# Edge stage of a graph-network kernel: every second group's one-hots on ScalarE, and a split first relu in every fourth pair

## The chip, the cores and the metric

The kernel runs on one core of one Trainium2 chip. The metric is the device time of one execution in microseconds (us). Engines are named as in the profile: PE is TensorE's matmuls, PEld its weight loads, DVE is VectorE, ACT is ScalarE, POOL is GpSimd, SP issues DMAs.

## The reference

3125 nodes with 256 features, 50,000 edges with 16 features. After a layer norm and a relu (giving h) comes a message-passing layer, then three graph convolutions, which the change doesn't touch. Cut to the part that it does touch:

```
h = maximum(layernorm(x), 0)
msg_input = concatenate([h[src], h[dst], edge_attr])      # 50000 x 528
hid       = relu(msg_input @ mW1 + mb1)                   # 50000 x 512
messages  = hid @ mW2 + mb2
aggregated = segment_sum(messages, src)                   # 3125 rows
```

Since the second matrix product is linear, the kernel sums hid over the edges of a source node first (the sums of this stage, 512 wide) and multiplies by mW2 once for each node later.

## The kernel before, in words

An earlier stage sorts the edges by source node, in blocks of 128 source nodes, and writes them as 440 tiles of 128 edges. It leaves A = h times the source part of mW1 plus mb1 in SBUF (each as two F32R halves whose sum is the value), and B = h times the target part in DRAM. F32R is the 32-bit type that PE reads with reduced precision; F32 operands go in full.

The edge stage (`edge_mlp`) works on pairs of tiles; both tiles of a pair belong to one source block. There are 220 pairs, and 110 quads of four tiles. For a pair p:

- one-hots (`one_hots`, L1188 to 1194): for a whole quad, one DVE is_equal makes `oh`, edge by source node, 128x512. It stands in even iterations, for the quad that PE needs two iterations later. There are four slots.
- turn (L1057): PE transposes the pair's two one-hots and its split edge features into PSUM; ACT copies them out (`turned` L1153, with a read of its accumulator, and `turned_e` L1155).
- edge (L1070): six matmuls with 512 columns sum the edge features' part and A's two halves in PSUM, over two PSUM areas in turns.
- pre (`add_target`, L1196 to 1207): DVE adds the rows of B, which POOL has gathered by indirect DMA, and writes `pre`, 128x1024 (512 for each of the two tiles).
- relus: the first tile's relu is written by ACT as F32 (`hid_whole`, L1161). The second tile's is split: ACT writes it rounded to F32R (`hid_upper`, L1165), and DVE subtracts that from the exact relu (`hid_lower`, `lower_part`, L1213).
- node (L1082): three matmuls sum by source node in `pNode`: the one-hot times `hid_whole` in F32 (L1087, two records of one pass pair each in the trace), times `hid_upper` (L1089) and `hid_lower` (L1091) in F32R.
- sums (`add_pair`, L1217 to 1226): DVE adds `pNode` to the block's running row sums. The block's place comes from a register; registers are loaded for four pairs at once, ahead of the sums in the iterations divisible by four.

All orders are written out by hand as loops over iterations i, one for each engine, and engines meet only by counting semaphores:

```
PE  (L1129): turn(i); edge(i-1); node(i-3)
ACT (L1148): turned(i), turned_e(i); hid_whole(i-2), hid_upper(i-2)
DVE (L1250): [i even: one_hots(i/2+1)]; pre(i-1); hid_lower(i-2); sums(i-4)
```

`pNode` has two buffers, so node(p) waits until sums(p-2) is done (`pe.wait_ge(sums_ready, p)`, L1085). By the loops above, node(i-2) in PE's iteration i+1 thus waits for the last operation of DVE's iteration i, whose first waits for edge(i-1) in PE's iteration i.

Of the kernel before, what the change touches and what calls it, by code (L numbers as in the profile page):

```python
# [5 lines left out]
P = 128  # L6
ALU = mybir.AluOpType
# [937 lines left out]
def edge_mlp(nc, io, dr, keep):  # L945


    with ExitStack() as stack:
# [3 lines left out]
        GRP = 4  # L952
        QUADS = NT // LC
        OHQ = 4
        WHOLE, SPLIT = 3, 2
        rows = g.sb("rows", [P, LCS, LC, ROW])
        rows_i = rows[:, :, :, :].rearrange("p s t w -> p (s t w)").bitcast(I32).rearrange(
            "p (s t w) -> p s t w", s=LCS, t=LC)
# [9 lines left out]
        whole = g.sb("hid_whole", [P, WHOLE, HID])  # L968
        upper = g.sb("hid_upper", [P, SPLIT, HID], F32R)
        lower = g.sb("hid_lower", [P, SPLIT, HID], F32R)  # L970
        ub2 = g.sb("ub2", [P, D])
        iota_i = g.sb("iota_cw_i", [P, CW], I32)
        ends_after = g.sb("ends_after", [P, NW])
        pair_m = g.sb("pair_m", [P, KP])
        col_f = brow[:, 0:2, :].rearrange("p s n -> p (s n)")[:, 0:2 * NT].rearrange("p (q t) -> p q t", q=2)
# [6 lines left out]
        cols_copied = g.sem("cols_copied")  # L982
        rows_in = [g.sem(f"rows_in{n}") for n in range(LCS)]
        b_in = [g.sem(f"b_in{n}") for n in range(BR)]
        oh_ready = g.sem("oh_ready2")
        turn_done = g.sem("turn_done")
        turn_copied = g.sem("turn_copied")
# [2 lines left out]
        whole_ready = g.sem("whole_ready")  # L990
        upper_ready = g.sem("upper_ready")
        lower_ready = g.sem("lower_ready")
        node_done = g.sem("node_done")
        sums_ready = g.sem("sums_ready")
        ub_in = g.sem("ub_in")
# [57 lines left out]
        def _(pe):  # L1053
# [2 lines left out]

            def turn(p):  # L1057
                q, j = divmod(2 * p, LC)
                pe.wait_ge(oh_ready, q + 1)
                if p >= 2:  # L1060
                    pe.wait_ge(turn_copied, p - 1)
                for n in range(2):
                    nc.tensor.transpose(pT[p % 2][:, n * P:(n + 1) * P], oh_upper[:, q % OHQ, j + n, :, 1],
                                        keep.ident16[:, :])
                for n in range(2):
                    last = nc.tensor.transpose(pT[p % 2][0:EW, (2 + n) * P:(3 + n) * P],  # L1066
                                               rows16[:, q % LCS, j + n, 4:4 + EW], keep.ident16[:, :])
                last.then_inc(turn_done, 1)
# [13 lines left out]
            def node(p):  # L1082
                q, j = divmod(2 * p, LC)
                if p >= 2:
                    pe.wait_ge(sums_ready, p)  # L1085
                pe.wait_ge(whole_ready, p + 1)
                mm(pN[p % 2][:, :], oh[:, q % OHQ, j, :].bitcast(F32), whole[:, p % WHOLE, :], start=True, stop=False)  # L1087
                pe.wait_ge(upper_ready, p + 1)
                mm(pN[p % 2][:, :], oh[:, q % OHQ, j + 1, :], upper[:, p % SPLIT, :], start=False, stop=False)  # L1089
                pe.wait_ge(lower_ready, p + 1)  # L1090
                mm(pN[p % 2][:, :], oh[:, q % OHQ, j + 1, :], lower[:, p % SPLIT, :], start=False, stop=True  # L1091
                   ).then_inc(node_done, 1)
# [52 lines left out]

        @block.scalar
        def _(act):
            for i in range(PAIRS + 2):  # L1148
                if i < PAIRS:
                    act.wait_ge(turn_done, i + 1)  # L1150
                    if i >= 2:
                        act.wait_ge(edge_done, i - 1)
                    nc.scalar.activation(turned[:, i % 2, :], pT[i % 2][:, 0:2 * P], ACT.Copy,  # L1153
                                         accum_out=keep.pair_deg[:, i:i + 1])
                    nc.scalar.copy(turned_e[:, i % 2, :], pT[i % 2][0:EW, 2 * P:4 * P]).then_inc(turn_copied, 1)  # L1155
                p = i - 2
                if p >= 0:
                    act.wait_ge(pre_ready, p + 1)
                    if p >= WHOLE:
                        act.wait_ge(node_done, p - WHOLE + 1)  # L1160
                    nc.scalar.activation(whole[:, p % WHOLE, :], pre[:, p % 2, 0:HID], ACT.Relu  # L1161
                                         ).then_inc(whole_ready, 1)
                    if p >= SPLIT:
                        act.wait_ge(node_done, p - SPLIT + 1)
                    nc.scalar.activation(upper[:, p % SPLIT, :], pre[:, p % 2, HID:2 * HID], ACT.Relu  # L1165
                                         ).then_inc(upper_ready, 1)
            act.wait_ge(edge_done, PAIRS)
            act.wait_ge(lists_done, 1)
            for m in range(KP):
                size = min(P, PAIRS - m * P)  # L1170
                nc.scalar.copy(keep.degT[0:size, m, :], pT32[0][0:size, m * P:(m + 1) * P]).then_inc(lists_copied, 1)
            act.wait_ge(lists_done, 2)
            full, size = KT - 1, NT - (KT - 1) * P
            for q in range(2):
                nc.scalar.copy(keep.turned_full(q),
                               pE[1][:, q * HID:q * HID + full * P].rearrange("p (m k) -> p m k", m=full)
                               ).then_inc(lists_copied, 1)
                nc.scalar.copy(keep.turned(q, full)[0:size, :], pE[1][0:size, q * HID + full * P:q * HID + KT * P]
                               ).then_inc(lists_copied, 1)
            act.wait_ge(lists_copied, KP + 4)  # L1180

        @block.vector
        def _(dve):
# [12 lines left out]
            def add_target(p):  # L1196
                dve.wait_ge(edge_done, p + 1)
                for t in (2 * p, 2 * p + 1):
                    dve.wait_ge(b_in[t % BR], 16 * (t // BR + 1))
                if p >= 2:  # L1200
                    dve.wait_ge(whole_ready, p - 1)
                    dve.wait_ge(upper_ready, p - 1)
                    dve.wait_ge(lower_ready, p - 1)
                at_row = (2 * p) % BR
                v.tensor_tensor(pre[:, p % 2, :], pE[p % 2][:, :],  # L1205
                                brow[:, at_row:at_row + 2, :].rearrange("p t n -> p (t n)"), ALU.add
                                ).then_inc(pre_ready, 1)

            def lower_part(p):
                dve.wait_ge(upper_ready, p + 1)  # L1210
                if p >= SPLIT:
                    dve.wait_ge(node_done, p - SPLIT + 1)
                v.scalar_tensor_tensor(out=lower[:, p % SPLIT, :], in0=pre[:, p % 2, HID:2 * HID], scalar=0.0,  # L1213
                                       in1=upper[:, p % SPLIT, :].bitcast(F32), op0=ALU.max, op1=ALU.subtract
                                       ).then_inc(lower_ready, 1)

            def add_pair(p):  # L1217
                if p % GRP == 0:
# [29 lines left out]

            one_hots(0)
            for i in range(PAIRS + 5):  # L1250
                if i % 2 == 0 and i // 2 + 1 < QUADS:
                    one_hots(i // 2 + 1)
                if 0 <= i - 1 < PAIRS:
                    add_target(i - 1)
                if 0 <= i - 2 < PAIRS:
                    lower_part(i - 2)
                if 0 <= i - 4 < PAIRS:
                    add_pair(i - 4)
# [935 lines left out]
```

## Time and profile before

| what | value |
|---|---|
| runs of the kernel | 2032.16, 2037.77, 2036.21 us; median 2036.21 us |
| the profiled execution | 2026.99 us |
| its span, first to last instruction | 2025.3 us |
| edge stage in it | from 546.5 us to about 1213 us |
| node matmuls in it, first and last weight load | 557.2 us and 1211.3 us |
| granted PE clock of the whole span, as a share of the full one | 0.925 |
| granted PE clock from 700 to 1200 us | 1.00 |
| busy in the whole span | PE 89%, DVE 76%, POOL 62%, PEld 61%, ACT 39% |

The profile is one execution, recorded by the hardware. "Busy" leaves out the time in which an engine waits. PE's matmul records overlap, since they are pipelined and their ends are modelled; how long a matmul holds the array is read from the starts of its neighbours and of the weight loads. DVE and ACT instructions also overlap the next one's start by a little, so that the step from start to start is shorter than the duration.

### The profile page before, as it was taken

Reading aid. Unit: us, or ns where it says so; the run is one execution under the profiler, and the core shown is the slowest. Engines: PE = TensorE matmul, PEld = TensorE weight load, DVE = VectorE, ACT = ScalarE, POOL = GpSimd, SP = SyncE. Lnnn points to the kernel's source line nnn. Section 1 sums busy time; section 2 is a strip of 40 time slices with the busy share of each in tenths; the row PEclk is TensorE's granted clock in tenths of the full one; section 3 lists DMA queues with packets and bytes.
Section 4 is the critical chain, followed back from the end, with each engine's and each line's share of the span. In section 5 each row is a group of like instructions: output and inputs, shape, how many; then the busy total and the mean of one; then the engine's idle time right before and its main releaser. Section 6 shows DMA issues by size and latency. Waiting matters only on the chain. (4 is left out here: it accounts for less than half of the span.)

```text
span 2025.3 us, 34940 instructions
## 1 busy us (share of the span) xinstructions
PE 1810.6 (89%) x9004; PEld 1239.8 (61%) x9005; DVE 1544.2 (76%) x4663; ACT 797.6 (39%) x1975; POOL 1256.3 (62%) x1468
## 2 busy tenths in 40 slices
PE   3577877777499999999999998999989999999999
PEld 3344444444255555555555556777758788888887
DVE  8877776777489999999999988999987445445333
ACT  0122222222155566665655555666664222103000
POOL 4777777777788888888888859999977100000000
PEclk7677777888699999999999999999999999999999
DMA  5111111111276666666666696222226233333333
GB/s 166 39 59 50 53 58 52 57 59 58 61 200 198 196 196 194 196 196 196 196 195 195 197 182 172 74 72 73 88 85 199 94 113 121 109 125 110 109 109 111
DMA packets 181291, 254.03 MB, mean 125 GB/s; under 512 B 28876, under 2 KB 144265, under 8 KB 181098
## 3 DMA queue, kind: packets, MB, share of 16 engines
q0 software_dynamic: 48048, 126.51, 22.7%
q1 hardware_dynamic: 104408, 102.03, 16.2%
q10 hardware_dynamic: 28642, 23.25, 3.6%
q8 instruction: 81, 1.33, 0.3%
q14 instruction: 112, 0.92, 0.2%
HBM read 202.22 MB, written 49.37 MB: 124 GB/s over the span
## 5 line engine op out<-in xcount | busy, mean ns | idle before, releaser
L1037 POOL DMA_INDIRECT brow<-B_rows,rows x440 | 470.0, 1068 | 115.2 <-issue 61.5
L393 POOL DMA_INDIRECT src_list<-ring,ring_row x392 | 385.4, 983 | 133.8 <-issue 116.8
L2018 PE MATMUL pO<-F,y 128*128 128x512 f32 x1728 | 427.7, 401 | 0.8 <-DVE y L1822 0.8
L2018 PEld LDWEIGHTS pO<-F,y 128*128 128x128 f32 x1728 | 325.1, 189 | 73.7 <-ACT zT L1911 1.5
L1360 POOL TENSOR_SCALAR src_oh<-iota,src_s 128x128 bf16<-128x128 bf16 x426 | 279.2, 672 | 32.4 <-PE pC L1512 15.8
L1087 PE MATMUL pNode<-hid_whole,oh 128*128 128x512 f32 x440 | 227.4, 598 | 4.2 <-DVE sums L1223 3.7
L1153 ACT ACTIVATE turned<-pC 128x256 fp32r<-128x256 bf16 x220 | 84.4, 384 | 280.4 <-PE pC L1066 280.4
L1376 DVE TENSOR_SCALAR dst_oh<-iota_cw,dst_s 128x458 bf16<-128x458 f16 x568 | 182.5, 370 | 1.6 <-PE pC L1512 1.4
L1512 PE MATMUL pC<-dst_oh,src_oh 128*128 128x458 bf16 x568 | 159.9, 361 | 18.4 <-SPq L1467 11.3
L1089 PE MATMUL pNode<-hid_upper,oh 128*128 128x512 f32 x220 | 174.9, 795 | 0.0
L852 PE MATMUL pP<-U,upto 128*128 128x182 bf16 x385 | 48.9, 277 | 136.4 <-DVE posf L612 136.4
L1205 DVE TENSOR_TENSOR pre<-pC,brow 128x1024 f32<-128x1024 f32 x110 | 134.7, 1225 | 45.2 <-PE pC L1078 41.6
L1078 PE MATMUL pC<-A,turned 128*128 x440 | 168.2, 493 | 0.0
L1078 PE MATMUL pSU<-A,turned 128*128 x440 | 167.1, 491 | 0.0
L1223 DVE SCALAR_TENSOR_TENSOR sums<-sums,going_on,pNode 128x512 f32 x220 | 163.6, 743 | 2.0 <-PE pNode L1091 1.2
L1818 DVE CAST F<-raw 128x512 fp32r<-128x512 uint16 x324 | 126.7, 432 | 32.4 <-PE pO L2018 32.0
L1213 DVE SCALAR_TENSOR_TENSOR hid_lower<-pre,hid_upper 128x512 fp32r<-128x512 f32 x220 | 151.4, 688 | 0.0
L1161 ACT ACTIVATE hid_whole<-pre 128x512 f32<-128x512 f32 x220 | 139.9, 636 | 7.4 <-DVE pre L1205 7.4
L1205 DVE TENSOR_TENSOR pre<-pSU,brow 128x1024 f32<-128x1024 f32 x110 | 134.2, 1220 | 5.1 <-PE pSU L1078 2.1
L1165 ACT ACTIVATE hid_upper<-pre 128x512 fp32r<-128x512 f32 x220 | 136.5, 620 | 0.0
L1595 ACT CAST c_rows<-pC 128x458 uint16<-128x458 f32 x175 | 94.6, 540 | 101.7 <-PE pC L1512 78.8
L852 PEld LDWEIGHTS pP<-U,upto 128*128 128x128 bf16 x385 | 36.0, 110 | 146.4 <-DVE posf L612 134.2
(308 smaller groups left out, 3423.6 us busy)
## 6 DMA issues: line engine op xcount, KB each, us to landing
raw<-C_rows SPq DMA_DIRECT2D x54, 768.0 KB, 4.3
C_rows<-c_rows ACTq DMA_DIRECT2D x175, 114.5 KB, 1.7
raw_first<-C_rows SPq DMA_DIRECT2D x18, 768.0 KB, 4.2
rows<-src_list SPq DMA_DIRECT2D x110, 100.0 KB, 2.8
brow<-B_rows,rows POOLq DMA_INDIRECT x440, 3.8
U_parts<-part_u SPq DMA_DIRECT2D x25, 256.0 KB, 2.0
B_rows<-bst SPq DMA_DIRECT2D x25, 256.0 KB, 2.1
src_list<-ring,ring_row POOLq DMA_INDIRECT x392, 2.2
```

The source lines that it names most:

```text
L393: nc.gpsimd.indirect_dma_start(dr.src_list[:, :, :].rearrange("p t w -> (p t) w"), bass.IndirectOffsetOnAxis(ap=ring_row[:, k % RING, t:t ...
L1037: nc.gpsimd.indirect_dma_start(brow[:, t % BR, :], None, dr.B, bass.IndirectOffsetOnAxis(ap=rows_i[:, m % LCS, j, 1:2], axis=0)).then_inc( ...
L1078: last = mm(to, turned[:, p % 2, n * P:(n + 1) * P], keep.A[:, 2 * HID + k * HID:][:, bass.ds(at[p], HID)], start=False, stop=(k == 1))
L1087: mm(pN[p % 2][:, :], oh[:, q % OHQ, j, :].bitcast(F32), whole[:, p % WHOLE, :], start=True, stop=False)
L1089: mm(pN[p % 2][:, :], oh[:, q % OHQ, j + 1, :], upper[:, p % SPLIT, :], start=False, stop=False)
L1205: v.tensor_tensor(pre[:, p % 2, :], pE[p % 2][:, :], brow[:, at_row:at_row + 2, :].rearrange("p t n -> p (t n)"), ALU.add).then_inc(pre_re ...
L1213: v.scalar_tensor_tensor(out=lower[:, p % SPLIT, :], in0=pre[:, p % 2, HID:2 * HID], scalar=0.0, in1=upper[:, p % SPLIT, :].bitcast(F32), ...
L1223: v.scalar_tensor_tensor(out=keep.sums[:, bass.ds(at[p], HID)], in0=keep.sums[:, bass.ds(at[max(p - 1, 0)], HID)], scalar=keep.going_on[:, ...
L1360: nc.gpsimd.tensor_scalar(src_oh[:, s % SLOTS, :], keep.iota16[:, :], src_s[:, s:s + 1], None, ALU.is_equal).then_inc(src_ready, 1)
L1376: v.tensor_scalar(dst_oh[:, s % SLOTS, :], iota_cw[:, :], dst_s[:, s:s + 1], None, ALU.is_equal).then_inc(dst_ready, 1)
L1512: mm(pC[:, bass.ds(at[s % GRP], CW)], src_oh[:, s % SLOTS, :], dst_oh[:, s % SLOTS, :], start=False, stop=False, skip_group_check=True).th ...
L2018: last = mm(pO[m % 2][half][:, :], y[:, win, part, half * P:(half + 1) * P], F[:, n % FS, :], start=(win == 0 and part == 0), stop=False)
```

## The change

It has three parts, all in `edge_mlp`.

1. Quads with an odd number get their one-hots from ACT. Four instructions (`distances`, two in each of two iterations) write the distance of the edge's source from each column, by the function Abs with the source number as a bias; one instruction on the quad's 512 columns (`own_one_hots`) makes relu(1 - distance) of it. They stand behind ACT's relus in the iterations 3, 0 and 1 modulo 4. DVE keeps the even quads, in the iterations 3 modulo 4.
2. In the pairs 3 modulo 4 the first tile's relu is split as the second's: ACT writes it rounded (`hid_upper_a`), DVE subtracts (`lower_part_a` to `hid_lower_a`), and node has four F32R matmuls in place of one F32 and two F32R.
3. `hid_whole` has two buffers instead of three, and the iota for later use lies in a part of `pre` that the second pair is the first to write.

```diff
-        WHOLE, SPLIT = 3, 2
+        WHOLE, SPLIT = 2, 2
+        BOTH = 4
...
-        iota_i = g.sb("iota_cw_i", [P, CW], I32)
+        iota_i = pre[:, 1, 0:CW].bitcast(I32)
...
             def turn(p):
                 q, j = divmod(2 * p, LC)
-                pe.wait_ge(oh_ready, q + 1)
+                if q % 2:
+                    pe.wait_ge(oh_own, (LC + 1) * (q // 2 + 1))
+                else:
+                    pe.wait_ge(oh_ready, q // 2 + 1)
...
-                pe.wait_ge(whole_ready, p + 1)
-                mm(pN[p % 2][:, :], oh[:, q % OHQ, j, :].bitcast(F32), whole[:, p % WHOLE, :], start=True, stop=False)
+                if p % BOTH == BOTH - 1:
+                    pe.wait_ge(whole_ready, p + 1)
+                    mm(pN[p % 2][:, :], oh[:, q % OHQ, j, :], upper_a[:, :], start=True, stop=False)
+                    pe.wait_ge(lower_a_ready, p // BOTH + 1)
+                    mm(pN[p % 2][:, :], oh[:, q % OHQ, j, :], lower_a[:, :], start=False, stop=False)
+                else:
...
+            def distances(q, t0):
+                act.wait_ge(rows_in[q % LCS], 16 * (q // LCS + 1))
+                if q >= OHQ:
+                    act.wait_ge(node_done, 2 * (q - OHQ) + 2)
+                for t in (t0, t0 + 1):
+                    nc.scalar.activation(oh[:, q % OHQ, t, :], keep.iota[:, :], ACT.Abs,
+                                         bias=rows[:, q % LCS, t, 0:1], scale=-1.0).then_inc(oh_own, 1)
+
+            def own_one_hots(q):
+                act.wait_ge(oh_own, (LC + 1) * (q // 2) + LC)
+                nc.scalar.activation(oh[:, q % OHQ, :, :], oh[:, q % OHQ, :, :].bitcast(F32), ACT.Relu,
+                                     bias=keep.ones[:, 0:1], scale=-1.0).then_inc(oh_own, 1)
...
+                if i == 0:
+                    distances(1, 0)
+                if i % 4 == 3 and (i + 3) // 2 < QUADS:
+                    distances((i + 3) // 2, 0)
+                if i % 4 == 0 and (i + 2) // 2 < QUADS:
+                    distances((i + 2) // 2, 2)
+                if i % 4 == 1 and (i + 1) // 2 < QUADS:
+                    own_one_hots((i + 1) // 2)
...
+            def lower_part_a(p):
+                dve.wait_ge(whole_ready, p + 1)
+                if p >= BOTH:
+                    dve.wait_ge(node_done, p - BOTH + 1)
+                v.scalar_tensor_tensor(out=lower_a[:, :], in0=pre[:, p % 2, 0:HID], scalar=0.0,
+                                       in1=upper_a[:, :].bitcast(F32), op0=ALU.max, op1=ALU.subtract
+                                       ).then_inc(lower_a_ready, 1)
...
-                if i % 2 == 0 and i // 2 + 1 < QUADS:
-                    one_hots(i // 2 + 1)
+                if i % 4 == 3 and (i + 1) // 2 < QUADS:
+                    one_hots((i + 1) // 2)
                 if 0 <= i - 1 < PAIRS:
                     add_target(i - 1)
                 if 0 <= i - 2 < PAIRS:
+                    if (i - 2) % BOTH == BOTH - 1:
+                        lower_part_a(i - 2)
                     lower_part(i - 2)
```

DVE's order, two iterations (i = 8 and 9) before the change. A line number L1192 is the one-hots, L1205 pre, L1213 hid_lower, L1223 sums (its ISA row sets up the register address):

```order
1697 L1192 TENSOR_TENSOR oh<-iota,rows 128x512 [waits node_done,rows_in3]
1698 L1205 TENSOR_TENSOR pre<-pSU,brow 128x1024 [waits whole_ready,upper_ready,b_in7,lower_ready,b_in6,edge_done]
1699 L1213 SCALAR_TENSOR_TENSOR hid_lower<-pre,hid_upper 128x512 [waits node_done,upper_ready]
1700 L80 TENSOR_LOAD pair_at
1701 L1223 ISA [waits sums_ready,node_done]
1702 L1223 SCALAR_TENSOR_TENSOR sums<-sums,going_on,pNode 128x512
1703 L1205 TENSOR_TENSOR pre<-pC,brow 128x1024 [waits whole_ready,upper_ready,b_in1,lower_ready,b_in0,edge_done]
1704 L1213 SCALAR_TENSOR_TENSOR hid_lower<-pre,hid_upper 128x512 [waits node_done,upper_ready]
1705 L1223 ISA [waits sums_ready,node_done]
1706 L1223 SCALAR_TENSOR_TENSOR sums<-sums,going_on,pNode 128x512
```

The same two iterations with the change (its line numbers: L1246 pre, L1262 hid_lower_a, L1254 hid_lower, L1272 sums):

```order
1696 L1246 TENSOR_TENSOR pre<-pSU,brow 128x1024 [waits whole_ready,upper_ready,b_in7,lower_ready,b_in6,edge_done]
1697 L1254 SCALAR_TENSOR_TENSOR hid_lower<-pre,hid_upper 128x512 [waits node_done,upper_ready]
1698 L80 TENSOR_LOAD pair_at
1699 L1272 ISA [waits sums_ready,node_done]
1700 L1272 SCALAR_TENSOR_TENSOR sums<-sums,going_on,pNode 128x512
1701 L1246 TENSOR_TENSOR pre<-pC,brow 128x1024 [waits whole_ready,upper_ready,b_in1,lower_ready,b_in0,edge_done]
1702 L1262 SCALAR_TENSOR_TENSOR hid_lower_a<-pre,hid_upper_a 128x512 [waits node_done,whole_ready]
1703 L1254 SCALAR_TENSOR_TENSOR hid_lower<-pre,hid_upper 128x512 [waits node_done,upper_ready]
1704 L1272 ISA [waits sums_ready,node_done]
1705 L1272 SCALAR_TENSOR_TENSOR sums<-sums,going_on,pNode 128x512
```

The one-hots ahead of pre are gone from the first of the two, and the new subtraction stands between pre and sums in the second.

ACT's order with the change, in the iterations i = 8 and 9 (L1168 distances, L1173 own_one_hots, L1181 and L1183 the copies, L1190 hid_upper_a, L1192 hid_whole, L1196 hid_upper; before, an iteration was the two copies and the two relus):

```order
338 L1181 ACTIVATE turned,pair_deg<-pC 128x256 [waits edge_done,turn_done]
339 L1183 COPY turned_e<-pC 96x256
340 L1192 ACTIVATE hid_whole<-pre 128x512 [waits node_done,pre_ready]
341 L1196 ACTIVATE hid_upper<-pre 128x512 [waits node_done]
342 L1168 ACTIVATE oh<-iota,rows 128x128 [waits node_done,rows_in1]
343 L1168 ACTIVATE oh<-iota,rows 128x128
344 L1181 ACTIVATE turned,pair_deg<-pC 128x256 [waits edge_done,turn_done]
345 L1183 COPY turned_e<-pC 96x256
346 L1190 ACTIVATE hid_upper_a<-pre 128x512 [waits node_done,pre_ready]
347 L1196 ACTIVATE hid_upper<-pre 128x512 [waits node_done]
348 L1173 ACTIVATE oh<-oh,ones 128x512 [waits oh_own]
```

The rows 342, 343 and 348 are added; the next row is the copy for turn(10), whose PE transposes read what row 348 writes.

## Rows read from the trace of the kernel before

**Rows 1.** Stretches: busy time of each engine, granted clock, DMA share and GB/s.
```profile
core 0: us, PE busy (x) PEld busy (x) DVE busy (x) ACT busy (x) POOL busy (x), PEclk, DMA share, GB/s
800.00:900.00 100.00, 100.00 (x477) 59.57 (x475) 93.31 (x120) 60.44 (x170) 82.08 (x89) 1.00 0.68 196
```

**Rows 2.** Waits from 700 to 1200 us: in total, times, longest.
```profile
ACT turned L1153 <- PE pC L1066: 200.6, 169, 1.7
PEld pNode L1087 <- DVE sums L1223: 10.2, 45, 0.7
```

**Rows 3.** Timeline, PE over one iteration: start, us, engine, line, operation.
```profile
902.33 1.02 PE L1087 MATMUL pNode<-hid_whole,oh 128*128 128x512 f32 x2
...
903.42 0.40 PE L1091 MATMUL pNode<-hid_lower,oh 128*128 128x512 f32 x1
...
903.66 0.29 PE L1063 MATMUL pC<-ident,oh 128*128 128x128 bf16 x2
...
903.89 0.38 PE L1076 MATMUL pC<-we_rows,turned_e 96*128 96x512 bf16 x1
...
905.28 1.02 PE L1087 MATMUL pNode<-hid_whole,oh 128*128 128x512 f32 x2
...
906.61 0.28 PE L1063 MATMUL pC<-ident,oh 128*128 128x128 bf16 x2
```

**Rows 4.** Timeline, DVE over an iteration, and the weight loads of the node behind it.
```profile
905.48 1.23 DVE L1205 TENSOR_TENSOR pre<-pC,brow 128x1024 f32<-128x1024 f32 x1 [0.44 <-PE pC L1078]
...
906.62 0.68 DVE L1213 SCALAR_TENSOR_TENSOR hid_lower<-pre,hid_upper 128x512 fp32r<-128x512 f32 x1
...
907.22 0.74 DVE L1223 SCALAR_TENSOR_TENSOR sums<-sums,going_on,pNode 128x512 f32 x1
...
907.88 0.69 DVE L1192 TENSOR_TENSOR oh<-iota,rows 128x512 fp32r<-128x512 f32 x1
...
908.01 0.40 PEld L1087 LDWEIGHTS pNode<-hid_whole,oh 128*128 128x128 f32 x2
...
908.23 1.02 PE L1087 MATMUL pNode<-hid_whole,oh 128*128 128x512 f32 x2
...
908.48 1.22 DVE L1205 TENSOR_TENSOR pre<-pSU,brow 128x1024 f32<-128x1024 f32 x1
```

**Rows 5.** Timeline, the next iteration, whose sums follow a register load.
```profile
909.61 0.69 DVE L1213 SCALAR_TENSOR_TENSOR hid_lower<-pre,hid_upper 128x512 fp32r<-128x512 f32 x1
...
910.29 0.75 DVE L1223 SCALAR_TENSOR_TENSOR sums<-sums,going_on,pNode 128x512 f32 x1
...
911.09 0.30 PEld L1087 LDWEIGHTS pNode<-hid_whole,oh 128*128 128x128 f32 x2 [0.20 <-DVE sums L1223]
...
911.63 0.19 PEld L1089 LDWEIGHTS pNode<-hid_upper,oh 128*128 128x128 f32 x1 [0.24 <-issue]
...
912.52 0.12 PEld L1063 LDWEIGHTS pC<-ident,oh 128*128 128x128 bf16 x2 [0.27 <-issue]
```

**Rows 6.** Timeline, ACT over one iteration.
```profile
904.09 0.38 ACT L1153 ACTIVATE turned<-pC 128x256 fp32r<-128x256 bf16 x1 [1.18 <-PE pC L1066]
...
904.72 0.64 ACT L1161 ACTIVATE hid_whole<-pre 128x512 f32<-128x512 f32 x1
...
905.25 0.62 ACT L1165 ACTIVATE hid_upper<-pre 128x512 fp32r<-128x512 f32 x1
```

**Rows 7.** ACT's groups by shape, whole span: count, busy us, mean ns, idle before.
```profile
L1153 ACT ACTIVATE turned<-pC 128x256 fp32r<-128x256 bf16 x220 | 84.4, 384 | 280.4 <-PE pC L1066 280.4
...
L442 ACT ACTIVATE part_u<-pT,ub 128x128 f32<-128x128 f32 x100 | 28.5, 367 | 185.5 <-PE pT L892 185.5
...
L490 ACT ACTIVATE A<-resid,nmr,rstd 128x256 f32<-128x256 f32 x25 | 15.0, 600 | 2.4 <-DVE nmr L677 2.4
...
L1171 ACT CAST sums<-pC 128x128 bf16<-128x128 f32 x1 | 0.2, 246 | 0.0
```

More of the change, by code:

```diff
@@ L970, in edge_mlp @@
         lower = g.sb("hid_lower", [P, SPLIT, HID], F32R)
+        upper_a = g.sb("hid_upper_a", [P, HID], F32R)
+        lower_a = g.sb("hid_lower_a", [P, HID], F32R)
         ub2 = g.sb("ub2", [P, D])
-        iota_i = g.sb("iota_cw_i", [P, CW], I32)
+        iota_i = pre[:, 1, 0:CW].bitcast(I32)
         ends_after = g.sb("ends_after", [P, NW])
@@ L984, in edge_mlp @@
         b_in = [g.sem(f"b_in{n}") for n in range(BR)]
+        oh_own = g.sem("oh_own")
         oh_ready = g.sem("oh_ready2")
@@ L992, in edge_mlp @@
         lower_ready = g.sem("lower_ready")
+        lower_a_ready = g.sem("lower_a_ready")
         node_done = g.sem("node_done")
@@ L1085, in node @@
                     pe.wait_ge(sums_ready, p)
-                pe.wait_ge(whole_ready, p + 1)
-                mm(pN[p % 2][:, :], oh[:, q % OHQ, j, :].bitcast(F32), whole[:, p % WHOLE, :], start=True, stop=False)
+                if p % BOTH == BOTH - 1:
[4 more added lines that the diff above has]
+                else:
+                    pe.wait_ge(whole_ready, p + 1)
+                    mm(pN[p % 2][:, :], oh[:, q % OHQ, j, :].bitcast(F32), whole[:, p % WHOLE, :],
+                       start=True, stop=False)
                 pe.wait_ge(upper_ready, p + 1)
@@ L1160, in _ @@
                         act.wait_ge(node_done, p - WHOLE + 1)
-                    nc.scalar.activation(whole[:, p % WHOLE, :], pre[:, p % 2, 0:HID], ACT.Relu
-                                         ).then_inc(whole_ready, 1)
+                    if p % BOTH == BOTH - 1:
+                        nc.scalar.activation(upper_a[:, :], pre[:, p % 2, 0:HID], ACT.Relu).then_inc(whole_ready, 1)
+                    else:
+                        nc.scalar.activation(whole[:, p % WHOLE, :], pre[:, p % 2, 0:HID], ACT.Relu
+                                             ).then_inc(whole_ready, 1)
                     if p >= SPLIT:
@@ L1199, in add_target @@
                     dve.wait_ge(b_in[t % BR], 16 * (t // BR + 1))
+                if p == 1:
+                    dve.wait_ge(consts, KT + 2)
                 if p >= 2:
```

## Prediction

> **What bounds the kernel now.** I looked first at the stretches. Between 800 and 900 us, in the middle of the edge stage, PE is busy all the time at its full clock, DVE 93%, ACT 60%, POOL 82% [rows 1]. By that PE is the bound and DVE close behind. The list of waits says whether they hold each other up: ACT waits for PE's transposes, which is slack, and the only wait of PE for another engine is node's first weight load for DVE's sums, 10.2 us over 45 times [rows 2]. That is small, so the third view is the timeline, to see how near the other nodes are to waiting.
>
> PE's iteration: node starts at 902.33, turn at 903.66, the next node at 905.28 [rows 3]. So node takes 1.33 us, turn and edge 1.62 us, a pair 2.95 us. Edge's six matmuls last from 903.89 to 905.28, 0.23 us for one F32R matmul with 512 columns; node's last, 903.42 to 903.66, takes 0.24 [rows 3]. The F32 matmul is the rest of node: 1.33 - 0.47 = 0.86 us.
>
> DVE's iteration [rows 4]: edge ends at 905.28, pre starts 0.20 us later at 905.48, hid_lower 1.14 us after that, sums 0.60 us later at 907.22, ended at 907.96. The load of the next node comes at 908.01, 0.05 us behind the end of sums, although PE's array is not free before 908.23. So **this load waits for sums in every iteration**; it costs nothing while it comes early enough. Where it comes late [rows 5], sums end at 911.04, the load is at 911.09, and turn stands at 912.52; less 1.33 us of node, the node began in effect at 911.19, 0.10 us behind its load. So a node can't begin before sums' end + 0.15 us. Counted from the end of edge: 0.20 + 1.14 + 0.60 + 0.74 + 0.15 = 2.83 us, and PE gets there after 2.95 us. The slack of this chain (edge, pre, hid_lower, sums, node) is **0.12 us**, though DVE then has up to 0.44 us idle elsewhere [rows 4].
>
> **The change part by part.** I reckon in groups of four pairs, of which there are 55; before, a group is 4 x 2.95 = 11.80 us, and about 0.02 more: in one iteration of four the one-hots let pre start 0.05 late (908.48, where edge ended at 908.23) and the register load puts sums 0.08 later (0.68 behind hid_lower, for 0.60), so that the node begins at 911.19 where PE alone would have it at 908.23 + 2.95 = 911.18 [rows 4, 5]; with the few hundredths by which such starts scatter I take 0.02.
>
> - PE, the split pair: one F32 matmul of 0.86 us becomes two F32R of 0.23 to 0.24. That takes away 0.39 us a group. The trace's row counts here. The Trainium skill (FP8 and Floating Point Precision, TensorE Precision Notes) says that true FP32 makes four passes; four of 0.235 would be 0.94 us, the saving 0.47, and the sum below would come to nothing. The row, with 0.86, disagrees a little and decides.
> - DVE, work: half of the one-hots go, two becoming one in a group, 0.60 us from start to start (907.88 to 908.48) [rows 4]; hid_lower_a has the shape and operands of hid_lower and takes its step, 0.60 us. DVE's work in a group stays the same.
> - DVE, place: the one-hots stood ahead of pre, in time that DVE would else have idled. hid_lower_a stands **behind pre and ahead of sums**, in the iterations 1 modulo 4. There the chain becomes 2.83 + 0.60 = 3.43 us against PE's 2.95: a stall of **0.48 us**, once a group, for node(p) with p = 3 modulo 4, which is the shortened one. Its input hid_lower_a is no further wait, as it is done before those sums. It could cost 0.60 if the slack were nothing and 0.36 if all of DVE's idle time counted as slack of this chain (0.44 less the 0.20 that the handing over takes, 0.24); I take 0.48, since rows 4 and 5 agree on it.
> - After the stall: take the end of edge as 0. The node begins at 3.43, lasts 0.94, the next edge ends at 5.99. The edge between ended at 2.95 and DVE is free at 0.20 + 2.40 + 0.60 = 3.20, pre starts there, its node could begin at 3.20 + 2.63 = 5.83, before 5.99. The next iteration has the one-hots: DVE is free at 5.60, pre starts at 6.20, its node at 8.83, and PE arrives at 8.94. In the fourth the register load adds 0.08: pre at 9.14, node at 11.85, and PE at 11.89. So no other stall follows, and the 0.02 of before go, as one-hots and register load no longer share an iteration.
> - ACT, distances: with a pointer bias and 128 columns, L442 is the nearest row, 0.37 us each [rows 7]. ACT idles 1.18 us ahead of each turned copy [rows 6], two hide there. Nothing.
> - ACT, own_one_hots: PE's turn waits for it. From turn to the copy 903.66 to 904.09, and hid_upper at 905.25 + 0.53 = 905.78, where it can begin [rows 3, 6]. Its price isn't in the trace. Below: 0.62, as hid_upper without a bias. Above: 0.62 + 0.22, as L490 with two pointers has 600 ns for the 384 of L1153 at the same 256 columns. I take 0.74: 0.62 and the 0.12 by which L442 (367, one pointer) is above L1171 (246) [rows 7]. It ends at 906.52, is seen by 906.57, and turn comes at 906.61 [rows 3]. At 0.84 it is seen at 906.67, and turn would be late by 0.06, or by 0.16 with the 0.10 that a late load costs. But it is the turn ahead of the stalled node, where PE would have stood anyway, and its edge may end 0.21 late before a later node feels it (at 3.16 for 2.95, pre then at 3.36, and 3.36 + 2.63 = 5.99). Nothing in either case. The Trainium skill (ScalarE: Activation LUTs, What ACT_TABLE_LOAD costs) gives 280 ns + 0.833 ns a column with a pointer bias, 0.71 us here; no run here shows it yet.
> - Buffers: hid_whole(p) with two buffers waits for node(p-2), which stands ahead of turn(p+2) in PE's order, for which ACT has waited already. Nothing. hid_upper_a and hid_lower_a come free four pairs later. The iota is read by DVE before the second pre. Row loads (SP) and gathers (POOL) follow pre as before; POOL has 18% idle. Beginning and end: some tenths.
>
> Sum: a group -0.39 + 0.48 - 0.02 = +0.07 us; 55 groups, **+3.9 us**. The profiled execution took 2026.99, its span 2025.3; I expect about 2030.9 and 2029.2. The median of the runs is 9.2 us above that execution; with the same 3.9 it becomes **2040.1 us**. A difference under 0.3%, 6.1 us, can't be told from no change here.
>
> **Rivals.**
>
> - A: PE's saving comes through whole. For it: PE is the busiest engine [rows 1], and the Trainium skill (Perfetto Trace Analysis, Identifying Performance Opportunities) advises to improve the most contended engine first. As a mechanism: DVE would do hid_lower_a in its idle time and sums would be in time. 55 x (0.39 + 0.02) = 22.6 us less, 2013.6. Against: the load 0.05 us behind sums in each iteration [rows 4]. Even with the subtraction at no cost, the node behind the short one stands at 0.20 + 2.63 = 2.83 us after an edge that PE leaves after 2.56, so that all but 0.12 us of the 0.39 would be lost again. Chance 0.06 for the whole, 0.07 for such a part (55 x 0.14 = 7.7 less, 2028.5).
> - B: slower, by own_one_hots on ACT. It decides from 0.89 us on (905.78 + 0.89 + 0.15 = 906.82, 0.21 behind the turn); every further tenth is a tenth a group, 5.5 us: at 1.0 us 2046, at 1.1 us 2052. The same would come of distances that start late, since their two waits stand ahead of all later copies. For it: turn has only 0.04 us to spare, and no row has this form. Against: the bound above is 0.84. Chance 0.19.
> - C: the change doesn't do what it says, the new wait being hidden by another order: excluded by the order of the instructions, which has hid_lower_a between pre and sums. No chance of its own.
>
> **How the numbers follow.** The forecast has 0.68. Its own range comes from the stall between 0.35 and 0.60 (6.6 us either way) and F32's price (0.86 or 0.94: -4.4), mostly 2034 to 2047; beyond 2042.3 it counts as slower, for which I give 0.14 of it, and 0.54 for no change. A adds 0.11 to faster and 0.02 to same, B 0.19 to slower. Faster 0.11, same 0.56, slower 0.33. The range takes in part of the small version of A and most of B: 2031 to 2051.
>
> **What would show it.** Right: PE's waits for sums rise from 10.2 us to about 0.5 us once every four pairs, some 26 us in the stage, all at the nodes with hid_upper_a; hid_lower_a steps 0.60 us; a group lasts 11.89 us; the first turn of an odd quad hardly waits for ACT. Wrong: groups of 11.5 us or less (A), or waits of turn for own_one_hots, with sums no longer the last (B).

## The result, and the profile after

| what | before | with the change |
|---|---|---|
| median of six runs | 2037.11 us | 2043.62 us |
| lowest, highest | 2032.16, 2040.74 us | 2039.49, 2045.91 us |
| the profiled execution | 2026.99 us | 2044.34 us |
| first turn to last sums in it (the stage, below) | 664.3 us | 674.2 us |
| ahead of it, behind it | 549.4, 811.6 us | 550.8, 817.7 us |

The kernel before was run three times more than stood ahead of the prediction. The change makes it slower: the ratio is 1.0045 with an interval of 1.0025 to 1.0066, or 5 to 13 us; the two medians differ by 6.5 us, 0.32%. The time lies 3.5 us above the forecast and in its range, but not in the likeliest of the three classes, no change. The two profiled executions differ by 17.4 us, of which 9.8 lie in the stage. What lies behind it the change doesn't touch: in the profiles of all kernels of this study it takes 811.6 to 818.3 us, in no order that goes with their edits. So the stage is what is compared below.

The stretch that answers to [rows 1], of the changed kernel (columns as there):

```profile
800.00:900.00 100.00, 97.94 (x466) 57.91 (x465) 93.76 (x118) 73.55 (x207) 82.65 (x88) 1.00 0.69 192
```

PE, which was busy all the time, now stands still for 2%. Its waits from 700 to 1200 us [rows 2]:

```profile
PEld pNode L1096 <- DVE sums L1272: 27.5, 42, 1.0
...
PEld pNode L1101 <- DVE sums L1272: 14.2, 42, 0.7
PEld pC L1071 <- ACT oh L1173: 11.2, 41, 0.3
```

The first line is the forecast stall: 42 times, once in every four pairs, always at the node with `hid_upper_a` (L1096), and 0.65 us each. That is how long no weights were loaded ahead of it; the array itself loses less, as the groups below show. The timeline around one, to lay beside [rows 4]:

```profile
905.32 1.23 DVE L1246 TENSOR_TENSOR pre<-pC,brow 128x1024 f32<-128x1024 f32 x1 [0.35 <-PE pC L1086]
...
905.61 0.71 ACT L1173 ACTIVATE oh<-oh,ones 128x512 fp32r<-128x512 f32 x1
...
906.46 0.12 PEld L1071 LDWEIGHTS pC<-ident,oh 128*128 128x128 bf16 x2 [0.27 <-ACT oh L1173]
...
906.47 0.68 DVE L1262 SCALAR_TENSOR_TENSOR hid_lower_a<-pre,hid_upper_a 128x512 fp32r<-128x512 f32 x1
...
907.06 0.69 DVE L1254 SCALAR_TENSOR_TENSOR hid_lower<-pre,hid_upper 128x512 fp32r<-128x512 f32 x1
...
907.67 0.74 DVE L1272 SCALAR_TENSOR_TENSOR sums<-sums,going_on,pNode 128x512 f32 x1
...
908.46 0.19 PEld L1096 LDWEIGHTS pNode<-hid_upper_a,oh 128*128 128x128 f32 x1 [0.64 <-DVE sums L1272]
...
909.49 0.12 PEld L1071 LDWEIGHTS pC<-ident,oh 128*128 128x128 bf16 x2 [0.28 <-issue]
```

`hid_lower_a` pushes hid_lower and sums back by one step (906.47 to 907.06, 0.59 us). sums end at 908.41, the load stands 0.05 us behind them, and the next turn 1.03 us behind the load (0.94 of a short node and 0.10 of a late load). `own_one_hots` ends at 906.32 and the turn's load follows at 906.46.

What was not forecast stands two iterations later, here with POOL's row beside DVE's:

```profile
911.32 1.23 DVE L1246 TENSOR_TENSOR pre<-pC,brow 128x1024 f32<-128x1024 f32 x1
...
912.27 0.74 POOL L1050 TENSOR_TENSOR resid<-resid,ub 128x256 f32<-128x256 f32 x1
...
912.46 1.10 DVE L1254 SCALAR_TENSOR_TENSOR hid_lower<-pre,hid_upper 128x512 fp32r<-128x512 f32 x1
...
913.49 0.73 DVE L1272 SCALAR_TENSOR_TENSOR sums<-sums,going_on,pNode 128x512 f32 x1
...
914.28 0.30 PEld L1101 LDWEIGHTS pNode<-hid_whole,oh 128*128 128x128 f32 x2 [0.48 <-DVE sums L1272]
```

POOL adds a row vector to a block of `resid`, once in eight pairs, 25 times in the stage. The addition is line L1050 (L1045 before), in POOL's loop over the gathers, which neither the change nor the prediction touches. hid_lower, which begins 0.19 us into that addition, takes 1.10 us instead of 0.68; sums and the node come late, and PE waits at a node that had no stall to expect. Before the change the same addition stands elsewhere, as POOL's timeline of the kernel before shows:

```profile
905.23 0.74 POOL L1045 TENSOR_TENSOR resid<-resid,ub 128x256 f32<-128x256 f32 x1
```

It begins 0.25 us ahead of pre (905.48, [rows 4]) and ends during it; neither takes longer for it. So it is from the fifth addition on; the fourth begins 0.23 us after pre does, and the first three stand beside a hid_lower that takes 0.94 to 1.16 us.

How often this strikes is read from the groups, each the distance between the weight loads of turn(i) and turn(i+4), i = 11, 15 and so on. There are 51; the table leaves out the last, which takes 11.83 us before and 12.79 with the change:

| groups of four pairs | how many | each, us |
|---|---|---|
| before | 45 | 11.83 |
| before, irregular ones (two with a long hid_lower) | 5 | 12.2 to 12.4 |
| with the change, hid_lower as ever | 26 | 11.89 |
| with the change, one hid_lower of 1.1 us | 24 | 12.21 |

So 50 x 0.06 = 3.0 us come from the order of the work, 24 x 0.32 = 7.7 from the additions, 2.0 must go off for the long groups that the kernel before has itself, and the last group brings 1.0: 9.7 us, where the stage has grown by 9.8. In that last group one pre starts after 1.31 us of idle time that the trace puts down to no engine; the cause wasn't found.

### The profile page after: what moved, and what is told of

Read it like the earlier page. It is cut to its first block and busy times, and to the rows that moved or that the text cites. A ratio compares the mean times of both kernels' runs of the same rounds, so it can differ in the third digit from the quotient of the medians.

```text
span 2042.7 us, 35325 instructions
## 1 busy us (share of the span) xinstructions
PE 1812.4 (89%) x9005; PEld 1240.8 (61%) x9005; DVE 1553.9 (76%) x4663; ACT 895.7 (44%) x2250; POOL 1265.3 (62%) x1468
## 5 line engine op out<-in xcount | busy, mean ns | idle before, releaser
L1042 POOL DMA_INDIRECT brow<-B_rows,rows x440 | 494.3, 1123 | 116.1 <-issue 78.2
L1101 PE MATMUL pNode<-hid_whole,oh 128*128 128x512 f32 x330 | 172.5, 604 | 4.7 <-DVE sums L1272 3.3
L1181 ACT ACTIVATE turned<-pC 128x256 fp32r<-128x256 bf16 x220 | 84.5, 384 | 194.4 <-PE pC L1074 194.4
L1272 DVE SCALAR_TENSOR_TENSOR sums<-sums,going_on,pNode 128x512 f32 x220 | 163.3, 742 | 2.8 <-issue 0.4
L1254 DVE SCALAR_TENSOR_TENSOR hid_lower<-pre,hid_upper 128x512 fp32r<-128x512 f32 x220 | 161.0, 732 | 0.0
L1246 DVE TENSOR_TENSOR pre<-pC,brow 128x1024 f32<-128x1024 f32 x110 | 134.5, 1223 | 29.0 <-PE pC L1086 25.1
L1104 PE MATMUL pNode<-hid_upper,oh 128*128 128x512 f32 x220 | 152.7, 694 | 0.0
L1246 DVE TENSOR_TENSOR pre<-pSU,brow 128x1024 f32<-128x1024 f32 x110 | 134.4, 1222 | 20.0 <-PE pSU L1086 13.6
L1196 ACT ACTIVATE hid_upper<-pre 128x512 fp32r<-128x512 f32 x220 | 136.4, 620 | 0.0
L1895 DVE SCALAR_TENSOR_TENSOR tmp<-pY,dis,bias_g 128x256 f32<-128x256 f32 (+1 forms) x50 | 24.2, 484 | 118.7 <-PE pY L2115 118.7
```

The source lines that it names most:

```text
L1042: nc.gpsimd.indirect_dma_start(brow[:, t % BR, :], None, dr.B, bass.IndirectOffsetOnAxis(ap=rows_i[:, m % LCS, j, 1:2], axis=0)).then_inc( ...
L1246: v.tensor_tensor(pre[:, p % 2, :], pE[p % 2][:, :], brow[:, at_row:at_row + 2, :].rearrange("p t n -> p (t n)"), ALU.add).then_inc(pre_re ...
L1272: v.scalar_tensor_tensor(out=keep.sums[:, bass.ds(at[p], HID)], in0=keep.sums[:, bass.ds(at[max(p - 1, 0)], HID)], scalar=keep.going_on[:, ...
```

## The experiments

In each, `...` leaves out what the diff of the change shows already. "Stage" and "group" are those above. The kernel before, run beside the first four, took 2034.51 us (median of 19), beside e5 to e8 2034.10 (of 31).

**e1: ACT's one-hots alone**, every first relu as before.

```diff
-                if p % BOTH == BOTH - 1:
+                if p % BOTH == NEVER:
```

The same condition is replaced in ACT's and DVE's loops.

> The changed kernel without its split pairs: ACT still makes the one-hots of the odd quads, but node(p) with p = 3 modulo 4 has its F32 matmul again and DVE no added subtraction. Theory 1 (the added subtraction delays sums, and sums gate the node): no stall, a group of four pairs at 11.80 us as PE alone gives it, time within 4 us of the kernel before, waits of node for sums a few us in all. Theory 2 (ACT's one-hots come too late for turn and cost the time): the slowdown stays, groups of 11.9 us, turn waiting 0.1 to 0.3 us for ACT once a group. Theory 3 (POOL's additions to resid, one in eight pairs, stretch a DVE subtraction when they fall beside it) says nothing of which it is, but where it falls beside hid_lower a group has 0.3 us more.

Measured: 2037.93 us, ratio 1.0013 (0.9999 to 1.0027). 27 groups take 11.83, as before the change; 12 with a long hid_lower 12.17, 11 with a long `oh` on DVE about 11.99; one between them 12.21. The turn waits for ACT as often as in the change (11.2 us, 41 times, 0.27 each), and a group of 11.83 shows that nothing comes of it: ACT's part is free, Rival B is out, and the additions to `resid` cost something already here.

**e2: the split alone**, all one-hots on DVE ahead of pre, as before.

```diff
-                if i % 4 == 3 and (i + 1) // 2 < QUADS:
-                    one_hots((i + 1) // 2)
+                if i % 2 == 0 and i // 2 + 1 < QUADS:
+                    one_hots(i // 2 + 1)
```

ACT's `distances` and `own_one_hots` are gone, and turn waits for DVE's one-hots alone.

> The changed kernel with all one-hots on DVE as before, and the split relu in every fourth pair. Theory 1, worked as the prediction did: behind the stall of 0.48 us the next iteration has one-hots ahead of pre, DVE is free at 3.20 and pre can start at 3.80 only, the node at 6.43 for PE's 5.99: a second stall of 0.44. A group lasts 3.43 + 0.94 + 1.62 to 5.99, 6.43, 9.38, 12.33 us, 0.5 us more than before, +28 us in all, some 2065 us. Theory of work alone (DVE has 93% of the time and the added 0.60 us in 11.8 fit in): DVE's work in a group is 11.4 us, so no change or a gain of up to 20 us.

Measured: 2057.07 us, ratio 1.0104 (1.0077 to 1.0131); groups of 12.36, the stage 25.2 us longer than before. The timeline, DVE and the node loads:

```profile
903.79 0.68 DVE L1251 SCALAR_TENSOR_TENSOR hid_lower_a<-pre,hid_upper_a 128x512 fp32r<-128x512 f32 x1
904.39 0.69 DVE L1243 SCALAR_TENSOR_TENSOR hid_lower<-pre,hid_upper 128x512 fp32r<-128x512 f32 x1
904.99 0.74 DVE L1261 SCALAR_TENSOR_TENSOR sums<-sums,going_on,pNode 128x512 f32 x1
905.65 0.69 DVE L1220 TENSOR_TENSOR oh<-iota,rows 128x512 fp32r<-128x512 f32 x1
905.78 0.19 PEld L1093 LDWEIGHTS pNode<-hid_upper_a,oh 128*128 128x128 f32 x1 [0.66 <-DVE sums L1261]
...
906.26 1.21 DVE L1235 TENSOR_TENSOR pre<-pSU,brow 128x1024 f32<-128x1024 f32 x1
...
908.00 0.74 DVE L1261 SCALAR_TENSOR_TENSOR sums<-sums,going_on,pNode 128x512 f32 x1
...
908.79 0.30 PEld L1098 LDWEIGHTS pNode<-hid_whole,oh 128*128 128x128 f32 x2 [0.61 <-DVE sums L1261]
```

The subtraction gives the first stall; the one-hots right behind those sums hold pre back and give a second (0.61), so that the split alone costs over 0.5 us a group. With every second quad's one-hots on ACT it is 0.06. The group was expected at 12.33, the time at some 2065 us.

**e3: the change, with sums(i-4) ahead of pre(i-1)** on DVE, out of the chain.

```diff
+                if 0 <= i - 4 < PAIRS:
+                    add_pair(i - 4)
                 if i % 4 == 3 and (i + 1) // 2 < QUADS:
                     one_hots((i + 1) // 2)
...
-                if 0 <= i - 4 < PAIRS:
-                    add_pair(i - 4)
```

> The changed kernel with sums(i-4) moved ahead of pre(i-1) on DVE, where it only needs node(i-4), done 1.6 us earlier. Nothing else moves. Theory 1: sums no longer stand behind edge, so the node never waits for them, the stall goes, and PE's saving of 0.39 us a group comes through: groups of 11.41 us (PE's own time), up to 11.5 if DVE (10.8 us of work in a group) now and then is late; 19 to 22 us less than before, about 2016 us. Theory 2 (ACT's one-hots): turn still waits for ACT, groups of 11.7 or more. If DVE's saturation is the bound: groups of 11.8.

Measured: **2011.27 us, ratio 0.9885** (0.9858 to 0.9912), the fastest of the study. The stretch, then the timeline:

```profile
800.00:900.00 100.00, 100.00 (x493) 62.35 (x491) 96.44 (x124) 77.99 (x221) 81.85 (x92) 1.00 0.71 204
```

```profile
902.89 0.73 DVE L1272 SCALAR_TENSOR_TENSOR sums<-sums,going_on,pNode 128x512 f32 x1
...
905.08 0.68 DVE L1262 SCALAR_TENSOR_TENSOR hid_lower_a<-pre,hid_upper_a 128x512 fp32r<-128x512 f32 x1
905.67 0.69 DVE L1254 SCALAR_TENSOR_TENSOR hid_lower<-pre,hid_upper 128x512 fp32r<-128x512 f32 x1
906.28 0.74 DVE L1272 SCALAR_TENSOR_TENSOR sums<-sums,going_on,pNode 128x512 f32 x1
906.46 0.19 PEld L1096 LDWEIGHTS pNode<-hid_upper_a,oh 128*128 128x128 f32 x1
906.69 0.39 PE L1096 MATMUL pNode<-hid_upper_a,oh 128*128 128x512 f32 x1
```

The node's load has no sums to wait for: those that it needs ended at 903.62, 2.8 us ahead of it. PE is busy all the time, and from the tenth group on every group takes 11.41 = 4 x 2.95 - 0.39, also the 20 in which an addition makes a DVE operation long. Six of the first nine are irregular (11.56 to 12.09, one 15.04, between 600 and 700 us); their cause wasn't found.

**e4: the change, with POOL adding one column instead of 256.**

```diff
-                    r = keep.resid[:, w, :]
-                    nc.gpsimd.tensor_tensor(r, r, ub2[:, :], ALU.add).then_inc(ub_added, 1)
+                    r = keep.resid[:, w, 0:1]
+                    nc.gpsimd.tensor_tensor(r, r, ub2[:, 0:1], ALU.add).then_inc(ub_added, 1)
```

> The changed kernel in which POOL adds one column of ub2 to resid instead of 256, so most of that addition is left out of the result. Theory 3: in the changed kernel all 25 additions fall beside a hid_lower, which then takes 1.10 us for 0.68; with one column they are too short for it, all hid_lower take 0.68, all groups 11.93 us as the others now, and the time falls by some 6 us, to about 2037. Otherwise (the long hid_lower have another cause): 25 of 1.10 us stay and the time stays at about 2043.

Measured: 2031.18 us, ratio 0.9986 (0.9972 to 1.0000). The addition takes 0.20 us, it has ended when hid_lower begins, and that takes 0.68. All groups but one (12.12) take 11.90, the stage 664.8, 9.3 less than with the change. Beside the change's ratio the whole is 0.6% or 12 us, where about 6 were expected; 24 x 0.32 = 7.7 of them are in the groups counted above and 0.9 in the last one, the rest isn't explained.

**e5: the change, with the addition one gather later** in POOL's order.

```diff
-                w, k = divmod(t - 4 * LC - 1, 4 * LC)
+                w, k = divmod(t - 4 * LC - 2, 4 * LC)
```

> The changed kernel in which each of POOL's 25 additions to resid stands behind the next tile's gather instead of this one's, so in the next pair, in an iteration (0 modulo 4) that has no one-hots ahead of pre; its result is the reference's. Theory 3: by the trace it should then begin some 0.3 us ahead of pre and end during pre, as it did in the kernel before, where neither operation got longer. No hid_lower of 1.1 us, all groups 11.90 us, stage 7 us shorter than with the change, time 0 to 4 us above the kernel before. If only the amount of work on POOL counts and not its place, nothing changes (2043).

Measured: 2037.60 us, ratio 1.0017 (0.9994 to 1.0039). For the first 30 groups the addition begins 0.28 us ahead of pre, as before the change, and they take 11.90. Then one group is disturbed (12.15), the next addition meets a hid_lower (12.20), and from then on it stands 0.27 us behind the start of `oh`, where eight groups take 12.12. So the whole work of the addition costs nothing in one place; but the place isn't held by the order alone.

**e6: the change without the subtraction.**

```diff
-                    pe.wait_ge(lower_a_ready, p // BOTH + 1)
-                    mm(pN[p % 2][:, :], oh[:, q % OHQ, j, :], lower_a[:, :], start=False, stop=False)
+                    mm(pN[p % 2][:, :], oh[:, q % OHQ, j, :], upper_a[:, :], start=False, stop=False)
...
-                    if (i - 2) % BOTH == BOTH - 1:
-                        lower_part_a(i - 2)
```

> The changed kernel without hid_lower_a on DVE: the fourth matmul reads hid_upper_a a second time, so PE's work is as in the change and the result of these tiles is wrong in the sum. Theory 1: the stall of 0.48 behind the subtraction goes, but node after the short one is then gated, since from the end of edge it takes 2.83 us through DVE and PE is there after 2.56: 0.27 us there and 0.05 at the next, where DVE's one-hots push pre. A group lasts 11.73 us, 0.17 less than 11.90, 0.10 less than before: of PE's 0.39 us only a quarter comes through. Where POOL's additions fall decides another 0 to 7 us. Rival (the subtraction's time is the whole loss): 11.41 us, as PE alone.

Measured: 2034.15 us, ratio 1.0003 (0.9985 to 1.0020). Groups of 11.74 where no addition meets a DVE operation, 12.00 with a long `oh` (13), 12.21 with a long hid_lower (11). Even at no cost for DVE the short node gives 0.09 us a group and not 0.39; the node waits for sums 111 times, 40.6 us, from 700 to 1200 us. It also shows the other encounter, here in its timeline:

```profile
713.56 0.74 DVE L1271 SCALAR_TENSOR_TENSOR sums<-sums,going_on,pNode 128x512 f32 x1
714.22 0.94 DVE L1230 TENSOR_TENSOR oh<-iota,rows 128x512 fp32r<-128x512 f32 x1
714.49 1.26 POOL L1050 TENSOR_TENSOR resid<-resid,ub 128x256 f32<-128x256 f32 x1
715.08 1.21 DVE L1245 TENSOR_TENSOR pre<-pC,brow 128x1024 f32<-128x1024 f32 x1
```

**e7: the kernel before, with only the move of sums** (the diff of e3, on `one_hots` as it stood before).

> The kernel before with the one move of sums ahead of pre and nothing of the change. Theory 1: PE's own time is the bound there, 11.80 us a group, where it now has 11.83 to 11.87: 1 to 4 us less than before. So the gain of the change with sums moved (23 us) comes from both together. Rival (the order was worth it alone): 15 to 20 us less.

Measured: 2025.78 us, ratio 0.9963 (0.9946 to 0.9980). All groups take 11.81, PE's own 4 x 2.95; 24 long hid_lower pass without effect. The stage is 661.4, 2.9 less than before, within what was expected; the rest of the 8 us lies outside the stage and isn't explained. Against e3, 0.40 us a group is missing: the split's.

**e8: the change, with the subtraction behind sums** and its matmul last in the node.

```diff
-                        lower_part_a(i - 2)
...
+                if 0 <= i - 2 < PAIRS and (i - 2) % BOTH == BOTH - 1:
+                    lower_part_a(i - 2)
```

pre also waits for the subtraction of two pairs before, whose input it overwrites.

> The changed kernel with hid_lower_a behind sums, its matmul the last of node, and a wait of pre for it two pairs later (its buffer). Theory 1: the shortened node isn't stalled; hid_lower_a is ready 3.28 + 0.15 us behind edge and its matmul wants it at 2.95 + 0.70. But pre of the next iteration starts at about 3.3 (DVE is busy, and it waits for the subtraction's end), its sums let the node begin at 5.93 where PE is there at 5.51: a stall of 0.4 just one node later. A group 11.8 to 11.85 us, as before; a quarter of the gain that sums ahead of pre gave at most. Rival (any order with sums ahead of the subtraction does it): 11.45.

Measured: 2042.35 us, ratio 1.0050 (1.0032 to 1.0068); groups of 12.00, or about 12.24 with a long `oh` or hid_lower. It was to be 11.80 to 11.85: right in the place of the stall, too low in its size. The timeline:

```profile
906.45 0.74 DVE L1276 SCALAR_TENSOR_TENSOR sums<-sums,going_on,pNode 128x512 f32 x1
907.11 0.68 DVE L1266 SCALAR_TENSOR_TENSOR hid_lower_a<-pre,hid_upper_a 128x512 fp32r<-128x512 f32 x1
907.25 0.19 PEld L1096 LDWEIGHTS pNode<-hid_upper_a,oh 128*128 128x128 f32 x1
...
907.93 1.23 DVE L1250 TENSOR_TENSOR pre<-pSU,brow 128x1024 f32<-128x1024 f32 x1
...
909.67 0.74 DVE L1276 SCALAR_TENSOR_TENSOR sums<-sums,going_on,pNode 128x512 f32 x1
...
910.46 0.30 PEld L1099 LDWEIGHTS pNode<-hid_whole,oh 128*128 128x128 f32 x2 [0.71 <-DVE sums L1276]
```

The short node's load is in time now (907.25), as meant. But the subtraction holds pre until 907.93, and the node behind stands at 910.46 with a wait of 0.71: the stall has moved by one iteration, as expected. The expectation had pre 3.3 us behind the end of edge and a stall of 0.4; pre comes after 3.42 (edge ends at 904.51), as it starts 0.14 us behind the subtraction's end. The iteration behind the short node takes 3.50 us for 2.95, a stall of 0.55, and the next one, which has the one-hots, 0.04 more than 2.95: with PE's 11.41, 12.00.

**e9 and e12: e3 with every second pair split**, and nearly all one-hots on ACT.

```diff
-        BOTH = 4
+        BOTH = 2
```

The lines that give ACT the one-hots of all quads but the first aren't shown.

> Sums ahead of pre as in e3, and then more of the same: every second pair is split, and ACT makes the one-hots of all quads but the first (all four distances in the odd iterations, the relu in the even ones, one iteration earlier than in the change). Theory 1: with sums off the chain PE's own time counts, four pairs at 4 x 2.953 - 2 x 0.39 = 11.03 us; DVE has 4 x 2.40 + 2 x 0.60 = 10.8 us of work and ACT 10.5, so all three are nearly full. 11.05 to 11.2 us a group, 12 to 20 us below e3, about 1995. Rival (DVE at 98% can't be kept fed, or ACT's odd iterations with four distances, 2.8 us, delay turned copies): 11.4 and more, no gain over e3.

> The kernel of e9 once more, since its first run fell on a chip where the kernel before takes 8% longer and where pre waited for the gathered rows of B. If this chip runs the kernel before in about 2035 us: theory 1 has 11.05 to 11.2 us a group and 1993 to 2001 us in all, 10 to 18 us below what e3 took; the rival (DVE, ACT or the gathers at the faster pace don't keep up, as pre's waits in e9 may show) 11.4 and more, 2011 us or above.

**e10: the change again. e11: the kernel before, with POOL adding one column.**

> The changed kernel as it is, once more beside the kernel before on the same chip. All that was found should show again: 24 or 25 hid_lower of 1.1 us, 11.89 us for the groups without one and 12.20 for those with, 7 to 11 us above the kernel before. If the place of POOL's additions differs from run to run, their number does, and the time with it.

> The kernel before in which POOL adds one column of ub2 to resid instead of 256 (most of that addition is left out of the result), the control for e4. Theory 3: in the kernel before only the first three additions fell beside a hid_lower, so 1 us is to be had. If removing POOL's work helps in itself, 6 to 12 us as in e4.

Beside these four the kernel before itself took 7 to 8% longer, 2196.74 us beside e9 to e11 and 2179.09 beside e12; the cause stays open, and each is compared only with the kernel before as it ran beside it. Measured: e9 2217.97, ratio 1.0089 (1.0062 to 1.0115); e12 2202.65, 1.0098 (1.0076 to 1.0119); e10 2202.16, 1.0024 (1.0009 to 1.0039), with 11 additions beside a hid_lower of 1.02 to 1.11 us; e11 2199.46, 1.0012 (0.9997 to 1.0027). The fastest groups of e9 and e12 are 11.02 and 11.01, what PE alone would need with two short nodes, but others reach 17, as DVE and ACT wait for something outside the engines (waits of e9 from 700 to 1200 us):

```profile
ACT turned L1181 <- remote: 59.6, 35, 4.4
DVE pre L1246 <- remote: 50.0, 34, 4.1
```

So what this version is worth where the kernel before takes 2035 us is open. e10 shows the change slower again, by less, with fewer additions beside hid_lower; but its groups take 12.2 to 13.6 us, not the 11.89 and 12.20 expected, and those of e11 11.8 to 13.6, so that what the additions cost can't be read from them. e11's expected gain of 1 us is less than its interval. Its rival, that leaving out POOL's work gains 6 to 12 us wherever it stands, would need a ratio of 0.9973 or less, and the interval (0.9997 to 1.0027) excludes that, in the slower condition.

## Why the prediction was right, and where not

- *The bound.* "This load waits for sums in every iteration": right. e7 and e3 take sums out of the chain and leave nothing but PE's own work, 11.81 and 11.41 us a group.
- *PE's saving, 0.39 a group.* Right: e3 against e7 gives 11.81 - 11.41 = 0.40. The row was the better guide than four passes (0.47).
- *The stall.* Right in place, cause and size. A group was to be 11.89 and is 11.89 on average in the 26 groups that no addition disturbs (11.85 to 11.93), 11.90 in e4. A stall is thus 11.89 - 11.41 = 0.48 us, as forecast. The sign named for it was less exact: "some 26 us in the stage" of waits was 55 x 0.48, but the wait in the trace is 0.65 each, 27.5 us from 700 to 1200 us alone and 36.2 in the whole stage, since the unit that loads weights stands idle for longer than the array does.
- *own_one_hots.* 0.74 was taken, and L1173 takes 0.714 on average, the distances 0.392 for 0.37; the Trainium skill (ScalarE: Activation LUTs, What ACT_TABLE_LOAD costs) gives 0.707 and 0.387 by its formula, and the trace agrees. The forecast that the turn "hardly waits" holds for the time, not for the list of waits: it shows 0.27 us in each group, as it does where no engine is named (`<-issue`), and e1 loses nothing by it.
- *Rival A, its small version.* "All but 0.12 us of the 0.39 lost again": e6 shows 11.74, a gain of 0.09.
- *The step that failed* is the sentence on the buffers: "Row loads and gathers follow pre as before; POOL has 18% idle. Nothing." It counts POOL's gathers and its idle share, and leaves out its rare addition to `resid`, which had stood beside pre and now stands beside hid_lower. That is 0.32 us in 24 groups, 7.7 us, twice the term that was forecast, and it takes the result over the bound of 0.3%: without it, e4 and e5 stand at 0.9986 and 1.0017. e4 removes it with the addition's size, e5 for 30 groups with its place. The Trainium skill states the rule that bears on it, and the prediction overlooked it (SBUF — State Buffer, Who interferes with whom): a DVE instruction with two SBUF inputs contends with a GpSimd instruction that reads SBUF, and one with at most one SBUF input, outside its two-port modes, does not. The trace agrees: hid_lower, with two, goes from 0.68 to 1.10 us and ends 0.55 behind the addition; pre, whose one input is in PSUM, stays at 1.23.
- *Luck.* The stage of the profiled execution grew by 9.8 us, where the sum had 3.9; that the medians differ by only 6.5, and so lie 3.5 above the forecast, isn't the sum's merit.
- *Why the addition moved* was not settled. Its place in POOL's order is unchanged. It began 0.92 to 0.95 us behind pre's start all 25 times, but which wait on POOL brings it there was only read, not tried apart from e5.

## What to carry to other kernels

With PE 100% busy, its work can still be worth nothing to shorten: where a weight load stands 0.05 us behind another engine's last operation in every iteration, that chain is the second bound, and its slack is about all that a saving can bring (here 0.12 us of slack and 0.09 gained, in e6). Take out of the chain what nobody needs so soon, as e3 does with sums, before shortening PE: the same split that costs 0.07 us a group then gives 0.40. And before moving work on a nearly full DVE, list POOL's rare operations as well as its frequent ones, and see which DVE operation each of them will meet.

## What the runs showed of the hardware beyond that

- Where DVE starts first, both sides pay. In e6 `oh`, begun 0.27 us ahead of the addition, takes 0.94 us instead of 0.69, and the addition 1.26 instead of 0.74. So it is in e3 and e5, and in the kernel before with the first addition, where hid_lower began 0.26 us ahead and took 0.94. The Trainium skill (SBUF — State Buffer, Who interferes with whom) has the side that starts second blocked and the first untouched; the rows of the changed kernel (hid_lower second, longer by 0.42, the addition as ever) fit it, these don't, since the first is 0.25 longer too.
- Eight per cent from one time to another: on the chip of e1 to e4 the kernel before later took 2196.74 us. Of what ran beside it, e11's profile has the part behind the stage at 815 us as always, but 676 instead of about 550 us ahead of it and 706 instead of 664 in it.
